# Float32r parts for the second product of an expert layer, and its first weights loaded tile by tile

## What is computed

```python
flat_idx = expert_indices.reshape(-1)
flat_w = expert_weights.reshape(-1)
order = jnp.argsort(flat_idx)
tok = order // top_k
tokens_per_expert = jnp.bincount(flat_idx, length=n_exp).astype(jnp.int32)
xs = xf[tok]
h = jax.nn.gelu(jax.lax.ragged_dot(xs, w1, tokens_per_expert), approximate=False)
ys = jax.lax.ragged_dot(h, w2, tokens_per_expert)
ys = ys * flat_w[order][:, None]
out = jnp.zeros_like(xf).at[tok].add(ys)
```

## Time and profile before

| | |
|---|---|
| median of 3 runs | 886.63 us (882.33 to 886.64) |
| the profiled execution | 893.05 us |
| its span in the profile | 891.4 us |
| TensorE busy | 821.3 us, 92% of the span |
| VectorE busy | 627.0 us, 70% |
| ScalarE busy | 517.2 us, 58% |
| GpSimd busy | 172.3 us, 19% |
| moved by DMA | 91.16 MB |

### The profile page before, as it was taken

One profiled execution on the slowest core, in us unless ns is written; L12 is line 12 of the kernel. 1 busy time (PEld: TensorE's weight loads), 2 busy tenths in 40 slices (PEclk: granted clock), 3 DMA queues, 4 the chain that ended last, 5 costly groups with the idle time before them and its releaser, 6 DMA issues.

```text
span 891.4 us, 14782 instructions
## 1 busy us (share of the span) xinstructions
PE 821.3 (92%) x4714; PEld 486.3 (55%) x4715; DVE 627.0 (70%) x1192; ACT 517.2 (58%) x685; POOL 172.3 (19%) x295
## 2 busy tenths in 40 slices
PE   9999999999988999999987999999999979993098
PEld 6543333333458899999954533333333457882098
DVE  5898888888773222224237888888889387988975
ACT  4557777777742122222134577777777667396985
POOL 3241111111156000000061242100001706200000
PEclk9999999999999999999998899999999999996599
DMA  8898556664363111111467783333440000000002
GB/s 294 186 273 248 97 165 163 178 178 123 110 218 110 35 35 35 35 35 36 135 191 182 197 253 82 71 74 76 84 85 2 1 1 1 0 1 0 0 25 71
DMA packets 66560, 91.16 MB, mean 102 GB/s; under 512 B 24134, under 2 KB 50630, under 8 KB 66502
## 3 DMA queue, kind: packets, MB, share of 16 engines
q1 hardware_dynamic: 59196, 67.83, 29.6%
q0 software_dynamic: 5584, 19.93, 6.6%
q10 hardware_dynamic: 1728, 2.75, 0.8%
HBM read 62.64 MB, written 27.44 MB: 101 GB/s over the span
## 4 chain that ended last, share of the span: by engine, by line
PE 74%; DVE 9%; ACT 7%; issue 3%; DMA 3%; SPq 2%; another core or an unknown queue 1%; POOL 1%; DVEq 0%; ACTq 0%; POOLq 0%
PE PS L2291 13%; PE PS L2259 13%; PE PS L2280 12%; PE PS L2450 9%; PE PS L2435 9%; PE PS L2391 2%; PE PS L2523 2%; PE PS L2305 1%; PE PS L2551 1%; PE PS L2556 1%; PE PS L2560 1%; PE PS L2242 1%; PE PS L2222 1%; PE PS L2205 1%
## 5 line engine op out<-in xcount | busy, mean ns | idle before, releaser
L1645 DVE TENSOR_REDUCE MX<-PS 128x1 f32<-128x512 f32 x512 | 321.2, 683 | 43.7 <-PE PS L2259 43.1
L1208 ACT ACTIVATE Pt<-PS 128x1024 f32<-128x1024 f32 x256 | 248.0, 1021 | 99.9 <-PE PS L2280 98.9
L2259 PE MATMUL PS<-KSt,BIG 96*128 96x512 bf16 x512 | 175.5, 384 | 3.5 <-DVE bias_row L1532 2.7
L2280 PE MATMUL PS<-BIG,KSt 99*128 99x512 bf16 x512 | 150.1, 379 | 2.0 <-ACT Pt L1208 1.4
L2291 PE MATMUL PS<-Pt,VS 128*17 128x512 f32 x1024 | 136.2, 598 | 0.0
L2259 PEld LDWEIGHTS PS<-KSt,BIG 96*128 96x128 bf16 x512 | 40.5, 97 | 143.7 <-DVE MX L1645 88.4
L1769 DVE COPY KSt<-PS 128x256 f32<-128x256 f32 x23 | 9.8, 425 | 110.3 <-PE PS L2422 110.3
L2435 PE MATMUL PS<-KSt,Pt 128*128 128x128 f32 x736 | 86.0, 275 | 0.9 <-issue 0.9
L2435 PEld LDWEIGHTS PS<-KSt,Pt 128*128 128x128 f32 x736 | 85.6, 192 | 2.1 <-issue 1.1
L2280 PEld LDWEIGHTS PS<-BIG,KSt 99*128 99x128 bf16 x512 | 49.3, 98 | 55.8 <-ACT Pt L1208 4.9
L867 POOL TENSOR_TENSOR MP<-MX,zrow 128x16 bf16<-128x16 f32 x32 | 7.0, 219 | 275.4 <-DVE MX L1645 275.4
(11 more groups left out here) (213 smaller groups left out, 1162.9 us busy)
## 6 DMA issues: line engine op xcount, KB each, us to landing
qk_parts<-BIG SPq DMA_DIRECT2D x64, 192.0 KB, 3.6
BIG<-in_w POOLq DMA_DIRECT2D x12, 1024.0 KB, 5.7
BIG<-qk_parts SPq DMA_DIRECT2D x32, 192.0 KB, 3.3
KSt<-qk_parts SPq DMA_DIRECT2D x32, 192.0 KB, 3.8
v_rows<-BIG SPq DMA_DIRECT2D x8, 544.0 KB
VS<-v_rows SPq DMA_DIRECT2D x32, 136.0 KB, 3.0
BIG<-qk_parts SPq DMA_DIRECT2D x32, 128.0 KB, 3.9
KSt<-qk_parts SPq DMA_DIRECT2D x32, 128.0 KB, 3.9
```

What stands on the lines that cost most here:

```text
L1208: act.activation(PP[:, 2 * (kc % 2) + half, :, :].rearrange("p h t -> p (h t)"), ST[half], ACT.Exp, scale=DK ** -0.5).then_inc(exp_done, 1)
L1645: dve.tensor_reduce(MX[:, g % 2, i % TB, i // TB:i // TB + 1], ring(i), AX.X, ALU.max, negate=True).then_inc(max_taken, 1)
L2259: pe.matmul(ring(i), QS[0:ROWS, g, h, qc * P:(qc + 1) * P], KS[0:ROWS, g, h, :], start=True, stop=True).then_inc(max_done, 1)
L2280: last = pe.matmul(ST[half][:, i * S:(i + 1) * S], KS[0:ROWS + PARTS, g, h, kc * P:(kc + 1) * P], QS[0:ROWS + PARTS, g, h, :], start=True, ...
```

## The change

1. The second product is made from float32r parts. w2 and the hidden rows are each split in a high part (a copy to float32r) and a low part (the value less its high part). The product is the sum of hidden high by w2 high, hidden high by w2 low and hidden low by w2 high: 24 matmuls of 256 columns in place of 8 float32 ones.
2. The parts of w2 are made once and kept for all 8 experts: W2H in the second half of BIG, W2L in the first. The loaded w2 also lies in the first half (W2), and each low part is written over it. GpSimd loads w2 of experts 0 to 3 in the second batch and of 4 to 7 in the third; there it also splits experts 0 to 3, one per group. Experts 4 to 7 are split behind attention, the high parts by ScalarE (6 and 7 in the tail, 4 and 5 behind it), the low ones by VectorE.
3. w1 is no longer kept. It is loaded from HBM per tile into Pt: tiles 0 and 1 by SP, the others by GpSimd, each once the first product two tiles back is done. VectorE's copies of w1 are gone; the additions of the bias on GpSimd stand behind these loads.
4. ScalarE makes the hidden rows' high part behind each half of the GELU, VectorE the low part, over the GELU's own result.
5. SP loads slot rows one tile further ahead, before the store.
6. As W2L fills the first half of BIG, layer 1's weights and context are loaded behind the last second product.

```diff
+        with nc.sbuf_tensor("W2L", [P, E * FC * D], F32R) as W2L, nc.sbuf_tensor("W2H", [P, E * FC * D], F32R) as W2H, \
+                nc.sbuf_tensor("over_stacks", [P, 8192], F32), nc.sbuf_tensor("HL", [P, 2176], F32R) as HL:
+            pass
+        with nc.sbuf_tensor("W2", [P, E * FC * D], F32) as W2:
             pass
...
+        W2_LATE = [(e, first) for e in (6, 7, 4, 5) for first in range(0, FC * D, 1024)]
...
-            for e in (6, 7):
-                load_w2(sp, e, w2_late)
-            sp.wait_ge(tro_done, EARLY)
-            load_w2(sp, 4, w2_late)
...
+            sp.wait_ge(pv_done, 4 * NG * B)
+            load_first_w1(0)
+            load_first_w1(1)
...
+            load_slots(1, 0, 2)
             with sp.Fori(0, (SLOT_TILES - 3) // 2) as m:
                 for q in range(2):
-                    load_slots(m + 1, q, None)
+                    load_slots(m + 1 + (q + 1) // 2, (q + 1) % 2, None)
                     store_results(m, q)
...
             for t in range(SLOT_TILES - 3, SLOT_TILES):
-                if t == SLOT_TILES - 2:
-                    sp.wait_ge(w1_staged, SLOT_TILES)
+                if t == SLOT_TILES - 1:
+                    sp.wait_ge(y_done, SLOT_TILES)
                     load_weight(sp, 1, 1, awk_in)
                     load_context(sp, 1, 0)
...
                 store_results(t // 2, t % 2)
-            sp.wait_ge(y_done, SLOT_TILES)
+            load_weight(sp, 1, 2, awv_in)
+            load_context(sp, 1, 1)
...
+            def split_w2(e):
+
+                gp.wait_ge(w2_in[0], 16 * NG)
+                for k in range(FC * D // 512):
+                    high, low, raw = high_w2(e, 512 * k, 512), low_w2(e, 512 * k, 512), raw_w2(e, 512 * k, 512)
+                    gp.tensor_scalar(high, raw, 1.0, 1.0, ALU.mult, ALU.mult).then_inc(w2_part, 1)
+                    gp.wait_ge(w2_part, e * (FC * D // 512) + k + 1)
+                    gp.tensor_tensor(low, raw, high.bitcast(F32), ALU.subtract).then_inc(w2_early, 1)
...
-                if last:
-                    load_w2(gp, g, w2_in)
-                elif not first:
-                    load_w1(NG * (n - 1) + g)
+                if 0 < n < 3:
+                    load_w2(NG * (n - 1) + g)
+                    if n == 2:
+                        split_w2(g)
...
+            for t in range(2, SLOT_TILES):
+                gp.wait_ge(h_done, 2 * t - 2)
+                load_w1(t)
+                for i in range(2 * t - 4, 2 * t - 2) if t < 2 + NT // 2 else ():
+                    gp.tensor_tensor(X[:, i, :], X[:, i, :], bias_row[:, :], ALU.add).then_inc(biased, 1)
...
+                    if layer == 0:
+                        k = i - EARLY
+                        high_late(6 + k // 4, k % 4 * 512, 512)
...
+            act.wait_ge(tro_done, NT)
+            for e, first in W2_LATE[4:]:
+                high_late(e, first, 1024)
...
-            stage_w1(0, 1, 0)
+            for i in range(4):
+                low_late(i)
             slots_turned(0, 0, 0)
             slots_turned(0, 1, 0)
+            for i in range(4, 8):
+                low_late(i)
+            low_hidden(0, 0, 0)
...
-                pe.wait_ge(gelu_done, 2 * n + 2)
+                pe.wait_ge(h_high, 2 * n + 2)
                 wait(pe, ys_ready, n - 1)
+                for r in range(2):
+                    for c in range(FC):
+                        pe.matmul(bank(4 + q)[:, 0:D], hidden_high(q)[:, c * P:(c + 1) * P],
+                                  (W2H, W2L)[r][:, bass.ds(e * (FC * D) + c * D, D)],
+                                  start=(c == 0 and r == 0), stop=False)
+                pe.wait_ge(h_low, 2 * n + 2)
                 for c in range(FC):
-                    last = pe.matmul(bank(4 + q)[:, 0:D], M["ht"][q][:, c, :],
-                                     W2[:, bass.ds(e * (FC * D) + c * D, D)], start=(c == 0), stop=(c == FC - 1))
+                    last = pe.matmul(bank(4 + q)[:, 0:D], hidden_low(q)[:, c * P:(c + 1) * P],
+                                     W2H[:, bass.ds(e * (FC * D) + c * D, D)], start=False, stop=(c == FC - 1))
                 last.then_inc(y_done, 1)
...
-            pe.wait_ge(w2_in, 16 * (E - 4))
-            pe.wait_ge(w2_late, 16 * 4)
+            pe.wait_ge(w2_early, EARLY_EXPERTS * FC * D // 512)
+            pe.wait_ge(w2_low, len(W2_LATE))
             expert_tile(0, 0, 0)
```

More of the change, by code:

```diff
@@ L249, in build_program @@
         scattered = sem("scattered")
-        w1_in = sem("w1_in")
-        w2_in = sem("w2_in")
-        w2_late = sem("w2_late")
+        w1_first = [sem(f"w1_first{q}") for q in range(2)]
+        w1_tile = [sem(f"w1_tile{q}") for q in range(2)]
+        w2_in = [sem(f"w2_in{h}") for h in range(2)]
+        w2_part = sem("w2_part")
+        w2_early = sem("w2_early")
+        w2_high = sem("w2_high")
+        w2_low = sem("w2_low")
+        h_high = sem("h_high")
+        h_low = sem("h_low")
         xs_in = [sem(f"xs_in{q}") for q in range(2)]
@@ L536, in build_program, with high_w2, low_w2, raw_w2 @@
         assert B * TB == NT and ROUTED == 2 * TB
-        def load_w2(eng, e, done):
-            eng.dma_start(W2[:, e * FC * D:(e + 1) * FC * D].rearrange("p (c n) -> p c n", c=FC),
-                          io["w2"][e].rearrange("(c p) n -> p c n", p=P)).then_inc(done, 16)
+        def high_w2(e, first, count):
+            at = e * FC * D + first
+            return W2H[:, at:at + count]
+        def low_w2(e, first, count):
+            at = e * FC * D + first
+            return W2L[:, at:at + count]
+        def raw_w2(e, first, count):
+            at = e * FC * D + first
+            return W2[:, at:at + count]
+        def hidden_high(p):
+            return XH[:, :, :].rearrange("p c t -> p (c t)")[:, 2048 + p * FF:2048 + (p + 1) * FF]
+        def hidden_low(p):
+            at = 0 if p else HIDDEN_AT
+            return HL[:, at:at + FF]
+        HIDDEN_AT = NG * TB * G * (DK + 1)
+        EARLY_EXPERTS = 4
+        W2_LATE = [(e, first) for e in (6, 7, 4, 5) for first in range(0, FC * D, 1024)]
         EARLY = 2 * TB
@@ L907, in batch, with load_w2, load_w1 @@
                         between(n, g, first, last)
[L908 to L919 removed]
+                if layer:
+                    over_batches(gp, layer, batch)
+                else:
+                    for n in range(B):
+                        batch(n, n == 0, n == B - 1)
+            def load_w2(e):
+                gp.dma_start(raw_w2(e, 0, FC * D).rearrange("p (c n) -> p c n", c=FC),
+                             io["w2"][e].rearrange("(c p) n -> p c n", p=P)).then_inc(w2_in[e // NG], 16)
+            def load_w1(t):
+                e = gp.value_load(expert_i[0:1, t:t + 1], min_val=0, max_val=E - 1)
+                gp.dma_start(M["w1"][:, t % 2, :, :], io["w1"].rearrange("e (c p) n -> e p c n", p=P)[e]).then_inc(w1_tile[t % 2], 16)
+            def split_w2(e):
[5 more added lines that the diff above has]
+                    gp.tensor_tensor(low, raw, high.bitcast(F32), ALU.subtract).then_inc(w2_early, 1)
+            def load_experts(n, g, first, last):
+                if 0 < n < 3:
+                    load_w2(NG * (n - 1) + g)
+                    if n == 2:
+                        split_w2(g)
+                elif last:
+                    pass
                 elif g == 0:
@@ L1229, in copy_turned, with high_late @@
                 act.activation(TT[:, i % 2, :], bank(source)[:, 0:D], ACT.Copy).then_inc(on_evac, 1)
+            def high_late(e, first, count):
+                act.wait_ge(w2_in[1], 16 * NG)
+                act.activation(high_w2(e, first, count), raw_w2(e, first, count), ACT.Copy).then_inc(w2_high, count // 512)
             def write_norm(some):
@@ L1778, in expert_tile @@
                     slots_turned(m, q, 2)
-                    stage_w1(m, q, 2)
+                if t is None or t + 1 < SLOT_TILES:
+                    low_hidden(m, q, 1)
                 if t == SLOT_TILES - 7:
@@ L2429, in hidden @@
                 pe.wait_ge(xst_ready, t + 1)
-                pe.wait_ge(w1_staged, t + 1)
+                if isinstance(t, int) and t < 2:
+                    pe.wait_ge(w1_first[t], 16)
+                else:
+                    pe.wait_ge(w1_tile[p], 16 * (m + (q + ahead) // 2))
                 for half in range(2):
```

59 lines of the change are left out of this document (25 added, 34 removed).

## The result

The changed kernel takes **873.55 us** (median of 4 runs, 871.50 to 875.18). The kernel before takes 885.5 us in four runs (882.33 to 886.64): the three of above and one more. The ratio is 0.9867, with a 95% interval from 0.9846 to 0.9889: 1.3% faster. The forecast was 876 us. The profiled execution of the changed kernel took 875.18 us with a span of 873.2 us.

A forecast was written before the change was run, and what follows sets the result against it. Expert layer bound by TensorE instructions, the stretch behind it by waits. -13.3 - 3.8 + 0 + 0 + 1.9 + 4.5 = -10.7 us, from 893.05 to 882.4 profiled, less 6.4 gives 876 us; range 870 to 881.

The forecast's parts named there:

- Term 1: Second product in the expert layer: 24 float32r pairs at 0.12 us replace 3.46 us; -13.3 us over 23 tiles.
- Rival D: Second product: a float32r pair costs only its columns, 0.108 us, so 2.6 us a product; time 869 us, chance 0.05.
- Term 2: Slot rows in the expert layer: loading one tile further ahead removes TensorE's late tiles; -3.8 us, bounds 0 and -3.8.
- Term 3: w1 loaded per tile in the expert layer: 7.2 of 9.8 us used, 2.6 us of cover; 0 us.
- Rival B: w1 arrives late, so every first product in the expert layer waits on HBM; 897 us at 9.3 us landing, chance 0.08.
- Term 4: GpSimd's w2 splits in the third batch: 8.8 of 9.66 us of waiting used; 0 us, upper bound +4.
- Term 5: Start of the expert layer: TensorE waits for VectorE's subtractions, hidden(1) at about 281.7; +1.9 us, bounds +0.6 and +3.
- Term 6: End of the expert layer: next layer's loads behind the last product make TensorE 4.7 us late, partly absorbed; +4.5 us.
- Rival A: End of the layer: loads, gathers and stores of parts share queues and cost 10 to 12 us; 882 us, chance 0.17.
- Rival C: Second product: per-matmul address register instructions run in series, 3.62 us a product, +3.7 instead of -13.3; 893 us, chance 0.06.

The follow-up runs named there:

- float32_product: Changed kernel with the second product in float32 again from raw values, the subtractions still running; 887.89 us, ratio 1.0027 to the kernel before.
- before_slots_ahead: Kernel before with only the slot rows loaded one tile further ahead; 890.31 against 894.34 us, ratio 0.9958.
- two_terms: Changed kernel without the eight matmuls of hidden low by w2 high in the second product; ratio 0.9668 to the kernel before.
- after_again: Changed kernel, unedited, measured and profiled again; 883.42 us, ratio 0.9885 to the kernel before.
- group 1: First of three groups of follow-up runs, each run beside the kernel before, which took 885.0 us in this one.
- slots_late: Changed kernel with slot rows loaded one tile less ahead and behind the store, as in the kernel before; 891.67 us, ratio 1.0065 to the kernel before.
- both_moved: Changed kernel with TensorE's w2-parts wait behind hidden(1) and layer 1's weights and context loaded two tiles earlier; 0.9786 of the kernel before, repeated 0.9806 (877.14 us).
- groups 2 and 3: The other two groups of follow-up runs, each beside the kernel before, which took 894.3 and 894.2 us in them.
- before_again: Kernel before, unchanged, profiled once more; 886.01 us.

## Why the prediction was right

The forecast was 876 us, the time 873.55; in differences -10.7 was forecast and -11.95 measured. The main gain, the shorter product with the slot rows ahead, came by the mechanism forecast. The two smaller terms at the ends of the layer are right in sum, and partly by luck. The parts:

- **Term 1** (second product, -13.3 us): -13.4 us in L by float32_product. 24 pairs at 0.12 us are 2.88 us, and the chain has 1.91 + 0.96. The page of the Trainium skill that I set against it ("FP8 and Floating Point Precision", TensorE Precision Notes) gives four passes for true float32; that the reduced form takes one is my reading of it. Counted so, the estimate was 2.6 us a product and -20 us. The trace is near it and not at it: a float32 matmul of 256 columns takes 0.43 us (3.46 / 8) and a float32r one 0.12, a ratio of 3.6 and not 4. The row of the same instruction in the same program was right to 0.01 us a product. Rival D is out.
- **Term 2** (slot rows, -3.8 us): right alone, by before_slots_ahead. As a term of this sum it hid something: with w1 under way it holds back 17.5 us. The terms 2 and 3 do not add: without the slot rows ahead L is 163.1 us, as long as before, and with an eighth of w1 it is 150.7 us. So it is w1's traffic, not the shorter product, that makes term 2 large. The sum came out right because both edits were in the change, so that TensorE waited for no load and the tile was the sum of its products.
- **Term 3** (w1 per tile, 0): right for w1 itself. Landing is 5.3 us and was taken as 5.7, L is 159.0 us with w1 from HBM and without (float32_product, before_slots_ahead), and two_terms finds the first waits with 1.9 of the 2.6 us of cover gone. What the step left out is that 1 MB per tile delays others: slot rows from 2.0 to 2.7 us, stores from 1.7 to 3.2. Term 2 covers it; without term 2 the 0 of term 3 would have been 12 us. Rival B was the wrong transfer to fear: not w1 comes late but the 128 KB beside it.
- **Term 4** (splits in the third batch, 0): GpSimd's wait is 2.1 us where 9.66 - 8.8 = 0.9 were forecast, and attention's exponentials span 190.6 us against 191.1 and 190.6 before. Leaving the splits out was not tried.
- **Term 5** (start, +1.9 us): S is 32.3 and 30.5 us in two profiles of the changed kernel against 29.6 to 30.4 in three of the old order: +0.1 to +2.7, around the 1.9. The subtractions took 1.155 us each, not 1.216. But the mechanism forecast is only part of it. From the last exponentials to hidden(1) it is 26.7 to 27.2 us in the seven profiles with the wait in its place, against 25.7 to 26.5 in the three of the old order: some 0.8 us later on average, and hidden(1) started at 280.34 and not at 281.7. The rest is a cause that the term did not have: a first product at reduced clock, +1.6 us, in both profiles of the changed kernel and in none of the three of the old order. In the first it hit hidden(1) and S has it in full; in after_again it hit hidden(0), ahead of the wait for the subtractions, and hidden(1) is no later for it. That the two profiles lie around 1.9 is luck.
- **Term 6** (end, +4.5 us): the keys are 4.0 us later (4.7 - 0.7), against 4.7 forecast. E is 2.1 us longer without the pause (66.3 to 68.4), 3.6 to 4.2 longer in the three variants of group 1 (69.9 to 70.5), and 4.2 with the pause (71.4 to 75.6). Moving the loads ahead gave 6.7 us in medians. Rival A, with 10 to 12 us, is out. The term was at the upper end of what is measured, and its argument was partly wrong: it leaned on the pause as if it were part of the kernel. The check that I had named, steady attention 3 to 6 us later after the last product, would have failed in the first pair of profiles (4.9 us earlier) for this reason alone.
- **Rival C** (register instructions in series) is out. Even where TensorE has lost its lead, in the late tile of slots_late, the first 16 pairs of the product take 2.14 us (309.34 to 311.48) against 1.98 in the next; 46 ns more for each would be 0.7 us.

Summed over the pair without the pause (spans 884.4 and 873.2): S +2.7, L -17.7, E +2.1, and +1.7 in all the rest, mostly a first attention that began 1.0 us later: -11.2 us. The forecast had +1.9, -17.1 and +4.5 for the three and nothing for the rest, so that misses of 1 to 2 us cancel. The measured medians have -11.95.

## What to carry to other kernels

Price a moved transfer in the traffic of the new kernel, not of the old one: a load that costs a tenth of a microsecond at a few borders costs most of a microsecond a tile when a megabyte per tile joins it (3.8 and 17.5 us over the layer), and an edit that looks like a small extra can be what the main gain stands on. Before explaining a difference in a stretch, profile both kernels in the same group of runs, and more than once; here the layer repeats everywhere, and the stretch behind it differs by 7 to 10 us between profiles of one and the same kernel (68.4 and 75.6, 70.5 and 80.4). Put a wait at the instruction that reads the data, and look whether a buffer's place in memory is what forces a load to be late.

## What the hardware showed that I had not expected

Near short idle times of TensorE a product can run at the lower clock, and which product is hit changes between executions of the same kernel. In the changed kernel it was hidden(1), 5.43 us behind 2.12 us of idle; in after_again it was hidden(0), behind an idle time of 0.90 us before the transposes and 0.56 after them:

```profile
274.76 5.44 PE L2508 MATMUL PS<-KSt,Pt 128*128 128x128 f32 x32 [0.56 <-issue]
280.65 3.81 PE L2508 MATMUL PS<-KSt,Pt 128*128 128x128 f32 x32 [0.45 <-issue]
```

The idle time alone does not decide: in slots_late hidden(1) took its 3.81 us behind 2.09 us of idle. And in both_moved_again, which has no wait between the two, the 64 matmuls took 9.01 us against 7.38 in both_moved:

```profile
275.61 9.01 PE L2508 MATMUL PS<-KSt,Pt 128*128 128x128 f32 x64 [0.39 <-issue]
```

Of seven profiles with the wait in its place, five show the slower product; of four with the wait moved, this one. So moving the wait removes the 2.1 us of idle but not, every time, the 1.6 us of clock.

Also not expected was that a pause of ScalarE of 5 to 11 us, booked to an unknown queue, is there in every profile of groups 2 and 3 and in none of group 1, while GpSimd's gathers and the stores of parts are under way in both. The code and the trace together say more than the name in the view. The two instructions of ScalarE that are held up in the first profile of before wait for semaphores of TensorE: L1062 for v_done alone, L1029 for qk_done (its other wait, for a store, is recorded as passed at 458.49 us). In before_again each update of the two is recorded 0.01 to 0.02 us after the end of the matmul that makes it. In the first profile of before the matmul that L1029 waits for has its end at 461.03 us and its update at 468.74, and that of L1062 has 461.89 and 471.58; in before_slots_ahead the first is at 458.01 and 467.37, in after_again at 450.87 and 453.72. So it is TensorE's signal that is late, by 3 to 10 us, and not a transfer. Why it is late stays open: the ends of matmuls are modelled in the trace, so the matmuls themselves may have been held up.
